# Normalising attention values from a copy in SBUF, and a seventh bank that serves every fourth maximum

## The reference, cut to what matters

```python
x = x + xattn(layernorm(x), ctx_768, Wq, Wk, Wv, Wo, bo)
x = x + ffn(layernorm(x), router_w, router_b, sw1, sb1, sw2, sb2, rw1, rb1, rw2, rb2)

def xattn(x, context, Wq, Wk, Wv, Wo, bo):
    q, k, v = ...                                   # 8 heads of 64
    attn = softmax(einsum('bhsd,bhld->bhsl', q, k) * 64 ** -0.5)
    out = einsum('bhsl,bhld->bhsd', attn, v)        # sum over 1601 keys, then / sum of exponentials
    return out.reshape(B, S, 512) @ Wo + bo
```

## Time and profile before

| | |
|---|---|
| median of 3 runs | 406.16 us (405.27 to 406.52) |
| the profiled execution | 405.86 us, its span 404.1 us |
| granted TensorE clock | 1.0 of full speed in the mean |
| PE busy | 395.5 us (98%) |
| VectorE (DVE) busy | 283.1 us (70%) |
| ScalarE (ACT) busy | 248.0 us (61%) |
| GpSimd (POOL) busy | 238.0 us (59%) |
| chain that ended last, by engine | PE 85%, ACT 4%, issue 4%, POOL 4%, DVE 3% |

### The profile page before, as it was taken

One profiled execution on the slowest core, in us unless ns is written; L12 is line 12 of the kernel. 1 busy time (PEld: TensorE's weight loads), 2 busy tenths in 40 slices (PEclk: granted clock), 3 DMA queues, 4 the chain that ended last, 5 costly groups with the idle time before them and its releaser, 6 DMA issues.

```text
span 404.1 us, 9723 instructions
## 1 busy us (share of the span) xinstructions
PE 395.5 (98%) x3718; PEld 330.4 (82%) x3718; DVE 283.1 (70%) x580; ACT 248.0 (61%) x400; POOL 238.0 (59%) x167
## 2 busy tenths in 40 slices
PE   8999999999999999999999999999999999999996
PEld 6787879797878887979789878888797877887886
DVE  3977898787646868878448687874586857567544
ACT  5678556382864654728837365468281945889782
POOL 6428568786902876447208782645074773588881
PEclk9999999999999999999999999999999999999999
DMA  6700002000000020000000220000000003203400
GB/s 190 202 1 2 2 2 63 2 2 3 0 2 2 3 62 3 2 2 0 3 2 3 63 58 2 0 2 2 2 3 0 2 3 113 98 0 91 146 1 28
DMA packets 17141, 11.77 MB, mean 29 GB/s; under 512 B 10188, under 2 KB 14136, under 8 KB 17096
## 3 DMA queue, kind: packets, MB, share of 16 engines
q1 hardware_dynamic: 17096, 11.15, 10.4%
HBM read 10.55 MB, written 0.56 MB: 27 GB/s over the span
## 4 chain that ended last, share of the span: by engine, by line
PE 85%; ACT 4%; issue 4%; POOL 4%; DVE 3%; DMA 1%; SPq 0%; DVEq 0%; ACTq 0%; POOLq 0%
PE ps L1197 21%; PE ps L1181 16%; PE ps L1028 9%; PE ps L1030 9%; PE ps L1029 9%; PE ps L1122 8%; PE ps L1172 6%; PE ps L1068 2%; PE ps L1129 2%; PE ps L1060 2%; ACT probs L802 1%; POOL kq_lo L704 1%; POOL work L486 1%; DMA raw<-in_ctx_T_dram 1%; ACT xn L725 1%
## 5 line engine op out<-in xcount | busy, mean ns | idle before, releaser
L923 DVE TENSOR_REDUCE maxes<-ps 128x1 f32<-128x402 f32 x256 | 132.6, 570 | 14.5 <-PE ps L1122 9.5
L802 ACT ACTIVATE probs<-ps 128x1024 f32<-128x1024 f32 (+1 forms) x112 | 105.5, 962 | 29.1 <-PE ps L1181 26.0
L486 POOL TENSOR_TENSOR work<-work,probs 128x1024 f32<-128x1024 f32 x45 | 107.4, 2386 | 3.5
L484 POOL TENSOR_TENSOR work<-probs 128x1024 f32<-128x1024 f32 x15 | 36.0, 2398 | 105.1 <-issue 89.4
L1197 PE MATMUL ps<-probs,v_sb 128*64 128x256 f32 (+1 forms) x832 | 93.4, 381 | 0.4 <-DVE work L866 0.4
L1197 PEld LDWEIGHTS ps<-probs,v_sb 128*64 128x64 f32 (+1 forms) x832 | 59.2, 137 | 30.7 <-issue 3.4
L1181 PE MATMUL ps<-kq_hi,kq_lo 64*128 64x256 f32 (+1 forms) x416 | 69.9, 280 | 0.0
L1181 PE MATMUL ps<-kq_lo,kq_hi 64*128 64x256 f32 (+1 forms) x416 | 69.9, 279 | 0.0
L1181 PE MATMUL ps<-kq_hi 64*128 64x256 f32 (+1 forms) x416 | 69.7, 279 | 0.0
L758 ACT COPY repeated<-rden 128x256 f32<-128x256 f32 x16 | 6.5, 405 | 90.0 <-DVE rden L902 90.0
L1122 PE MATMUL ps<-kq_hi 64*128 64x402 f32 x256 | 60.1, 366 | 0.1
(11 more groups left out here) (153 smaller groups left out, 694.5 us busy)
## 6 DMA issues: line engine op xcount, KB each, us to landing
v_sb<-weight_rows SPq DMA_DIRECT2D x12, 256.0 KB, 4.2
raw<-in_ctx_T_dram SPq DMA_DIRECT2D x3, 600.4 KB, 5.0
work<-in_L_ffn_rw_dram SPq DMA_DIRECT2D x1, 1024.0 KB, 7.7
shift_rows<-neg_row SPq DMA_DIRECT2D x64, 0.5 KB, 2.0
raw<-weight_rows SPq DMA_DIRECT2D x4, 256.0 KB, 3.5
raw<-in_ctx_T_dram SPq DMA_DIRECT2D x3, 150.8 KB, 2.8
x_sb<-in_x_dram SPq DMA_DIRECT2D x1, 384.0 KB, 6.6
wo_sb<-in_L_xattn_Wo_dram SPq DMA_DIRECT2D x1, 256.0 KB, 7.0
```

Source lines behind the costliest of these rows:

```text
L486: ops.tensor_tensor(acc, acc, pr, ALU.add).then_inc(summed, 1)
L802: nc.scalar.activation(dst, src, ACT.Exp, scale=SCALE).then_inc(probs_ready, 1)
L923: v.tensor_reduce(maxes[:, p % 2, i * T + t, blk:blk + 1], src[:, 0:BW], AX.X, ALU.max).then_inc(ring_taken, 1)
```

## The change: what it does

- `plan` puts two maxima in front of the scores of a pair instead of three, and two behind each unit: 2 + 14 are all sixteen. Before it was 3, then 2 behind six units and 1 behind the last.
- The maxima whose head and tile are (1, 1), every fourth, land in bank 7 instead of the ring's banks. The other twelve go round banks 4, 5 and 6.
- To make bank 7 free, ScalarE copies `o_bank` to `unscaled` in SBUF as soon as the row sums' reciprocals are there, in front of the repeated copy. The copy of the spread (`inverse`) goes, and VectorE multiplies `sums_bank` by `unscaled`.
- The spread waits for the reduction of the sixteenth maximum (`behind`), since it uses the same bank. It moves behind the first two projections; in pair 14, which has none, it moves behind the ring steps, just in front of the values. In pair 15 it stays behind unit 1.

```diff
-        out += ahead[:3]
+        out += ahead[:2]
         for u in range(n_units):
             out.append(("scores", (b, p, u)))
-            out += ahead[2 * u + 3:2 * u + 5]
+            out += ahead[2 * u + 2:2 * u + 4]
...
-        if 0 < n < n_order - 1:
-            out.append(("spread", order[n - 1]))
+        spread = [("spread", order[n - 1])] if 0 < n < n_order - 1 else []
+        if projections:
+            projections = projections[:2] + spread + projections[2:]
...
+        if not projections:
+            out += spread
...
-            bank = min(range(lowest, O_BANK), key=lambda i: held.get(i, -1))
+            with_o = w[0] == "max" and n > kinds.index("scores") and w[3:5] == (1, T - 1)
+            bank = O_BANK if with_o else min(range(lowest, O_BANK), key=lambda i: held.get(i, -1))
...
+    with_o = [k for k, bank in enumerate(ring_banks) if bank == O_BANK]
...
                     if pair:
-                        act.wait_ge(spread_filled, pair)
+                        act.wait_ge(sums_taken, pair)
+                    nc.scalar.copy(unscaled[:], o_bank).then_inc(o_copied, 1)
                     nc.scalar.copy(repeated[:], ...
-                elif kind == "spread":
-                    pair = w[0] * PAIRS + w[1]
-                    act.wait_ge(spread_filled, pair + 1)
-                    if pair:
-                        act.wait_ge(sums_taken, pair)
-                    nc.scalar.copy(inverse[:], sums_bank).then_inc(inverse_ready, 1)
...
-                dve.wait_ge(inverse_ready, pair + 1)
+                dve.wait_ge(spread_filled, pair + 1)
...
-                v.tensor_tensor(oT[:, b % 2, p, :], o_bank, inverse[:], ALU.mult).then_inc(sums_taken, 1)
+                v.tensor_tensor(oT[:, b % 2, p, :], sums_bank, unscaled[:], ALU.mult).then_inc(sums_taken, 1)
...
                 pe.wait_ge(repeated_ready, b * PAIRS + p + 1)
+                behind = [ring_list[k] for k in with_o if ring_list[k][1] * PAIRS + ring_list[k][2] <= b * PAIRS + p + 2]
+                pe.wait_ge(*taken(behind[-1]))
...
+                        if k in with_o and pair >= 2:
+                            pe.wait_ge(o_copied, pair - 1)
...
                         if u == 0 and pair:
                             pe.wait_ge(*sums_done(*divmod(pair - 1, PAIRS)))
+                        elif u == 0:
+                            pe.wait_ge(*taken(("max", 0, 1, 1, T - 1, BLOCKS - 1)))
```

More of the change, by code:

```diff
@@ L281, in build @@
         rden = sb("rden", [P, 2, T])
-        inverse = sb("inverse", [P, S])
+        unscaled = sb("unscaled", [P, S])
         repeated = sb("repeated", [P, T, 2, DH])
@@ L399, in build @@
         sums_filled, sums_taken = sem("sums_filled"), sem("sums_taken")
-        spread_filled, inverse_ready = sem("spread_filled"), sem("inverse_ready")
+        spread_filled, o_copied = sem("spread_filled"), sem("o_copied")
         repeated_ready = sem("repeated_ready")
```

## The result

The changed kernel takes 413.15 us in the median of 4 runs (412.06 to 413.38) against 406.0 for the kernel before (405.27 to 406.52, 4 runs). The ratio is 1.0172, with a 95% interval of 1.0148 to 1.0196: 7.1 us slower. The forecast was 411.1, with 408.6 to 413 as its own range and 407.0 to 414.0 as the range of all. The profiled execution has a span of 411.5 us, 7.4 more than before.

The account below looks back on a forecast made before the run. PE, busy 98% of the span, was taken as the bound. Terms 1.9 + 0.36 - 0.15 + 2.8 gave +4.9 on 405.86, so 410.8, or 411.1 us for the median; own range 408.6 to 413, overall 407.0 to 414.0.

Parts of the forecast that it names:

- pair 14: Spread behind two rings of VectorE's work: product late, values start 3.05 later, 0.24 returned, +2.8 us.
- ordinary pairs: Ten pairs (1, 2, 3, 5, 6, 7, 9, 10, 11, 13): two late waits, +0.19 each, +1.9 us.
- pairs 4, 8 and 12: Value projections between: gain 0.5 at first projection, pay 0.64 for the inserted spread; +0.12 each, +0.36 us.
- Exponential 5 and the sixteenth reduction: End of scores: ScalarE's exponential of unit 5 ends at 8.00, VectorE's last maximum reduction at 9.20 after pair start.
- the 0.45 gained before: Stage of scores: without unit 0's stall, exponential 5 ends 0.45 earlier; VectorE's last reduction comes no earlier.
- Pair 0: Has no spread: its exponential 5 comes 0.1 to 0.2 earlier, -0.15 us.
- Costed at nothing, the copy: ScalarE's new copy of the values, 0.37, covered by 0.33 before exponential 0; up to 0.37 per pair otherwise.
- Rival A: Gain passes through: 0.45 at exponential 5 reaches the values in 14 pairs, -6.3 + 2.8, about 402.7 us; chance 0.07.
- Rival B: A wash: reductions end 0.1 to 0.2 earlier, 13 pairs gain, pair 14 eats it; 405.3 to 407.3 us; chance 0.10.
- Rival C: Matmuls on the same array half cost 0.06 at 14 borders, 0.6 a pair, +9, about 420 us; chance 0.06.

Follow-up runs that it names:

- runs with the queries first: Changed kernel, pair 14's spread before its rings, queries' projection before first keys' projection: 407.76 us; with the spread also behind the second keys' projection: 402.43 us.
- run with the repeated spread: Changed kernel with the four spread matmuls in front of pair 14's values issued six times over; 411.73 us, ratio 1.0143.
- the couples alone: Kernel before with two maxima in front and two behind each unit, banks 4 to 6 for all, no copy of the values; 405.98 us, ratio 0.9997.
- the first experiment: Changed kernel with pair 14's spread directly behind the scores, in front of the rings xt and wrow; 408.39 us, ratio 1.0064.

## Why the prediction was right, and where it was off

The way and the mechanism came out as forecast: the waits, their places and their ends are in the trace. What the forecast did not have is the clock in pair 14. The size came out short, +7.1 us where +4.9 was summed, and 413.15 lies just above the forecast's own range of 408.6 to 413. Two of the errors in the sum cancel, and that is luck: ordinary pairs lost 0.5 more than summed, pairs 4, 8 and 12 together 0.5 less.

- **Exponential 5 and the sixteenth reduction.** Predicted to end at 8.00 and 9.20, measured 7.98 and 9.16. The first projection's second matmul: 8.41 predicted, 8.39 measured; the third projection's: 9.98 and 10.01. That the 0.45 gained before is spent again, on a wait for exponential 5 and on one more maximum behind the last unit, is shown by the runs with the queries first: the first wait filled alone gave nothing, both filled gave 0.5 a pair.
- **Ordinary pairs** were summed at 0.19 and lost 0.24. Eight of them lost 0.22 in the mean. Pairs 6 and 10 lost 0.35: in them ScalarE normalises tokens between exponentials 2 and 3, exponential 5 comes only 0.3 earlier (in pair 6 it ends at 8.56, before at 8.90), the reductions end at 9.74 and 9.76 (before at 9.58 and 9.59), and the spread waits for them. I had not worked these two out apart.
- **Pairs 4, 8 and 12** were summed at +0.12 each (0.64 less 0.5 is 0.14, a slip that changes nothing) and gave -0.04. The mis-sized term is the price of the spread as an insertion, 0.64 from a place where PE turns from half-height to full-height matmuls. Inside a stream of projections it is 0.45: in pair 4 after the change it starts at 110.80, and the second matmul behind it comes at 111.48, where it would have been at 111.03.

```profile
110.80 0.61 PE L1070 MATMUL ps<-ident,repeated 128*128 128x128 f32 x4
111.17 0.48 PE L1028 MATMUL ps<-wv_hi,ctxT_hi 96*128 96x512 f32 x1
111.48 0.40 PE L1029 MATMUL ps<-wv_lo,ctxT_hi 96*128 96x512 f32 x1
```

- **Pair 0** was to gain 0.15 and gained nothing: exponential 5 ended 8.12 after the start, as before (8.11). Its unit 0 lasts 1.22 with two in front as with three, where pair 7's lasts 1.12 in the changed kernel. The rows place the difference at the first shift, which starts behind idle time: the first score matmuls come 0.31 behind it, in pair 7 of the changed kernel 0.22. Why they do stays open.
- **Pair 14** is the term that was off: +2.8 predicted, +4.39 measured. The wait itself was nearly right, 3.05 against 3.16: the sixteenth reduction ends 0.14 later than before in this pair (9.74, before 9.60), where the sum took 0.09, and its own figures (9.20 against 9.15) give 0.05. The step that failed is "the values' first matmul waits for this product, and everything on PE is behind it. Of that 0.24 is returned": it let the values run in their old 5.84 us. Behind PE's 2.94 us of idle time the clock was halved, and they took 7.52. The run with the repeated spread puts 1.4 us on it by the median, 1.69 by the pair's length. What is returned was about 0.45, not 0.24, since the sums no longer wait for VectorE's additions and start before the modelled end of the values: 3.16 + 1.68 - 0.45 is 4.39.
- **Costed at nothing, the copy:** right, 1.0006 (0.9994 to 1.0018). The 0.33 of cover that the prediction summed measured 0.42.
- **Rival A**, the gain passing through, is not what the change did, but a good part of it is to be had: with the spread as cover and no wait for the sixteenth reduction ordinary pairs gain 0.29 of the 0.45, and the kernel takes 401.3 us. The rival said 402.7 with 2.8 of loss in pair 14, which is 399.9 without. **Rival B** did not happen. **Rival C**, matmuls on the same half of the array in a row, is excluded: in pair 7 of the changed kernel units 0 and 1 last 1.12 and 1.13, no more than the 1.14 of the earlier trace rows. Of the two conditions that the Trainium skill gives for weights pulled ahead ("TensorE: Matmul & The Clock Gate", Step-by-step: what each phase is for), the second, the background buffer, is the one that fits.
- **A premise was wrong**, though no number hung on it: I gave the removal of unit 0's stall to the bank as much as to the maximum less in front. Either alone is enough. With two in front and three banks the stall is gone (the couples alone have a unit 0 of 1.12, and without the bank the first experiment's kernel takes 408.59 us against 408.39), and with three in front and the bank it is gone too (402.4 us, unit 0 of 1.12).

## What to carry to other kernels

A stall that is removed early in a stage is worth what the next wait leaves of it: before moving a step, look up what waits for it and what it covers. Here the spread was the cover of the wait for exponential 5, and giving its bank to the last maximum of the stage put a second wait behind the first. When a scarce resource is shared, share it with an item that is done early (maximum 13, not 16), and do not place a short step behind the long queue of the engine that consumes it.

## What the runs showed of the hardware that I had not expected

PE had been at full clock for over 300 us. Then it stood idle for 2.94 us, after 0.40 of idle time in front of the four small matmuls before, and about 1 us after it had taken up work again the granted clock fell from 1.0 to 0.50, where it stayed for over 3 us. This cost 1.7 us. Six times the same four small matmuls in that stretch kept it at 1.00 and made the kernel faster (411.73 against 413.15 us). The idle stretch of 1.55 us in pair 14 of the first experiment did not lower it: the values behind it took 5.83.
